# Self-attention in 32x32 diagonal blocks, with the block transposes on VectorE

## Chip, cores and metric

The kernel runs on one core of a Trainium2 chip. The metric is the device time of one execution in microseconds (us), as the median of several.

## What is computed

A pre-norm decoder layer on x of 16 x 128 x 1024 (2048 tokens), all fp32: self-attention, cross-attention with a context, and a feed-forward product, each added to its input. Only the self-attention matters here. It runs over the first axis, 16 long, so each of the 128 positions is a causal sequence of 16 tokens of its own:

```python
def _L0_attn_ref(tokens, weight_qkv, weight_proj):   # tokens: 16, 128, 1024
    NUM_HEADS, NUM_KV_HEADS, HEAD_DIM = (32, 8, 128)
    scale = 1.0 / HEAD_DIM ** 0.5
    qkv = jnp.einsum('sbh,ph->sbp', tokens, weight_qkv)
    ...
    k = jnp.repeat(k, Q_PER_GROUP, axis=2)           # 4 query heads share one k and one v
    v = jnp.repeat(v, Q_PER_GROUP, axis=2)
    ...
    scores = jnp.einsum('bhsd,bhtd->bhst', q, k) * scale
    causal = jnp.tril(jnp.ones((S, S), dtype=bool))
    scores = jnp.where(causal, scores, jnp.finfo(scores.dtype).min)
    attn = jax.nn.softmax(scores, axis=-1)
    out = jnp.einsum('bhst,bhtd->bhsd', attn, v)
    out = out.transpose(2, 0, 1, 3).reshape(S, B, NUM_HEADS * HEAD_DIM)
    return jnp.einsum('sbe,he->sbh', out, weight_proj)

x = x + _L0_attn_ref(_layernorm(x, axis=-1), L0_attn_weight_qkv, L0_attn_weight_proj)
```

## The kernel before

The 2048 tokens are laid out so that the 16 tokens of a sequence are neighbours. They form 4 blocks of 512, each of 4 tiles of 128 tokens; a tile holds 8 sequences. Of the 128x128 scores of a tile and head only 8 diagonal blocks of 16x16 are wanted; the mask `causal` sets the rest to -1e30.

`self_attention_phase` is a software pipeline of 33 steps (`pipeline`, line 271): a block has 8 groups (one k, one v and four q heads), and step n projects group n while it does the attention of group n-1. Step 0 has no attention, step 32 no projection. Inside a block, steps run two at a time in a hardware loop. Each engine has its own instruction list, written out by hand in `step`, and semaphores tie them together. The parts of a step:

- `unit(u)`, u from 0 to 5: projection of k, v and the four q heads for 512 tokens into the PSUM pair `u_ps`, 8 chunks of 128 features with three matmuls each. All large products are done in three passes (`three_passes`, line 48): an fp32 operand is split into a high part (rounded to fp32r) and a low part (the remainder), and high x high, high x low and low x high are summed.
- The splits: ScalarE (ACT) copies a weight tile to its high part (`weights`, line 598; `out_weights`, line 647), GpSimd (POOL) subtracts to get the low part (lines 436 and 447). POOL's order in a step: four splits of output weights (`sa_pl`, line 450), the projection weights of units 3, 4, 5 of this step, and those of units 0, 1, 2 of the next (`sa_wl`, line 439). `unit(u)` waits for its split on `w_split` (line 484).
- `scores(t)`, tile t: four plain fp32 matmuls of 128x128 into bank `s_ps` (line 521).
- `softmax(t)` on VectorE (DVE), lines 735 to 752: mask, maximum, subtract, then exp on ACT (`exps`, line 655), sum, reciprocal, multiply, 512 elements each in `probs`.
- `turn_probs(t)`: four 128x128 transposes on TensorE (PE) into bank `t_ps` (line 531), split by ACT (line 665) and DVE (line 756) into `probsTh` and `probsTl`.
- `mix_values(t)`: the product with v in three matmuls into `o_ps`; its split is `high_o` on ACT (line 671) and `low_o` on DVE (line 761), in one buffer `oh`/`ol`.
- `project(t)`: output projection of 4 heads, 2 halves of 512 columns, 24 matmuls, added to `acc` by DVE (`add_projected`, line 768). It needs all four output weight splits (`p_split`).
- `turn_v` transposes v (line 496); `fold_half` prepares weights of cross-attention (line 507).

The order on PE (lines 558 to 589) places a pair of turn and scores between the units, and `project(0)`, `mix_values(1)`, `turn_probs(2)` and `scores(3)` between `turn_v` and `unit(3)`. On ACT (lines 673 to 701) `out_weights([0, 1])` stands before `exps(0)`.

Of the kernel before, what the change touches and what calls it, by code (L numbers as in the profile page):

```python
# [13 lines left out]
P = 128  # L14
# [15 lines left out]
SELF_SCALE = 1.0 / HD ** 0.5  # L30

# [12 lines left out]
def f32(ap):  # L44
    return ap.bitcast(F32)
# [18 lines left out]
def constants_phase(nc, sems, ident, causal, pairmask, mix, bias_qkv, eps, b_nat, inter_rows, amp_col):  # L64

    with ExitStack() as ctx:
# [13 lines left out]
        slotmask = sb("slotmask", [P, SLOTS])  # L80
        bias_ps = ctx.enter_context(nc.psum_tensor("bias_ps", [P, HALF], F32))
# [15 lines left out]
        def _(pool):  # L97
# [9 lines left out]
                               pattern=[[-1, P]], channel_multiplier=1).then_inc(masks_built, 1)  # L107
# [7 lines left out]
            pool.affine_select(out=cv, in_=cv, compare_op=ALU.is_ge, fill=MASKED, base=SEQ - 1,  # L115
                               pattern=[[SEQ, P // SEQ], [0, SEQ]], channel_multiplier=-1).then_inc(masks_built, 1)
# [6 lines left out]
        def _(dve):  # L123
# [5 lines left out]
                                    ALU.add).then_inc(mix_steps, 1)  # L129
            dve.wait_ge(small_loaded, 48)  # L130
# [162 lines left out]
def self_attention_phase(nc, sems, ident, causal, mix, eps, x_rows, wqkv, wproj, w_nat, w_folded, x1):  # L293
# [7 lines left out]
    with ExitStack() as ctx:  # L301
# [22 lines left out]
        probs = sb("sa_probs", [P, QPG, P])  # L324
        probsTh = sb("sa_probsTh", [P, QPG * P], F32R)
        probsTl = sb("sa_probsTl", [P, QPG * P], F32R)
        top = sb("sa_top", [P, QPG])
        total = sb("sa_total", [P, QPG])
        inv = sb("sa_inv", [P, QPG])
        oh = sb("sa_oh", [P, QPG * P], F32R)  # L330
        ol = sb("sa_ol", [P, QPG * P], F32R)
# [5 lines left out]
        s_ps, t_ps, o_ps, v_ps = bank("sa_s"), bank("sa_t"), bank("sa_o"), bank("sa_vt")  # L337
        turn_ps = [s_ps, t_ps, o_ps, v_ps]
# [20 lines left out]
        inv_done = sem("sa_inv_done")  # L359
        probs_ready = sem("sa_probs_ready")  # L360
        probs_turned = sem("sa_probs_turned")
        probsT_hi = sem("sa_probsT_hi")
        probsT_ready = sem("sa_probsT_ready")
# [68 lines left out]
        def _(pool):  # L432
            pool.sem_inc(w_split, 3)
            pool.sem_inc(p_split, QPG)

# [26 lines left out]
        def _(pe):  # L462
            pe.sem_inc(pr_done, 1)
            pe.sem_inc(folded, 2)

# [9 lines left out]
            def step(s):  # L475
# [36 lines left out]
                def scores(t):  # L512
                    if not s.attn:
                        return
                    if t == 0:
                        pe.wait_ge(u_copied, n * U + 2)
                        if s.cross:
                            pe.wait_ge(ln.lo_done, s.b * ln.GROUPS + 5)
                    pe.wait_ge(s_masked, m * TILES + (t + 1))
                    for h in range(QPG):  # L520
                        ins = nc.tensor.matmul(s_ps[:, h * P:(h + 1) * P], qT[:, mp, h, t * P:(t + 1) * P],
                                               kT[:, mp, t * P:(t + 1) * P], start=True, stop=True)
                    ins.then_inc(s_done, 1)

                def turn_probs(t):
                    if not s.attn:
                        return
                    pe.wait_ge(probs_ready, m * TILES + (t + 1))
                    pe.wait_ge(probsT_ready, m * TILES + (t + 1))
                    for h in range(QPG):  # L530
                        ins = nc.tensor.transpose(t_ps[:, h * P:(h + 1) * P], probs[:, h], ident[:])
                    ins.then_inc(probs_turned, 1)

                def mix_values(t):
                    if not s.attn:
                        return
                    if t == 0:
                        pe.wait_ge(v_copied, v0 + 1)
                    pe.wait_ge(probsT_ready, m * TILES + (t + 2))
                    pe.wait_ge(o_split, m * TILES + (t + 1))  # L540
                    three_passes(nc, o_ps[:], [(vh[:, mp, t], vl[:, mp, t], probsTh[:], probsTl[:])]
                                 ).then_inc(o_done, 1)

                def project(t):
# [4 lines left out]
                    pe.wait_ge(o_split, m * TILES + (t + 2))  # L549
                    for half in range(2):  # L550
# [3 lines left out]
                                           [(oh[:, h * P:(h + 1) * P], ol[:, h * P:(h + 1) * P],  # L554
# [3 lines left out]
                scores(0)  # L558
                unit(0)
                turn_probs(0)  # L560
                scores(1)
                unit(1)
                mix_values(0)
                turn_probs(1)
                scores(2)
                unit(2)
                turn_v()
                project(0)
                mix_values(1)
                turn_probs(2)  # L570
                scores(3)
                unit(3)
                fold_half(0)
                project(1)
                mix_values(2)
                turn_probs(3)
                unit(4)
                fold_half(1)
                project(2)
                mix_values(3)  # L580
                unit(5)
                if s.norm:

                    pe.wait_ge(o_split, m * TILES + (TILES + 1))
                    pe.wait_ge(v_copied, v0 + 4)
                    turn_groups(s.b + 1, range(4))
                project(3)
# [6 lines left out]
        def _(act):  # L594
# [15 lines left out]
            def step(s):  # L610
# [44 lines left out]
                def exps(t):  # L655
                    if not s.attn:
                        return
                    act.wait_ge(s_shifted, m * TILES + (t + 1))
                    nc.scalar.activation(probs[:], probs[:], ACT.Exp, scale=SELF_SCALE).then_inc(exp_done, 1)

                def copy_probs(t):
                    if not s.attn:
                        return
                    act.wait_ge(probs_turned, m * TILES + (t + 1))
# [1163 lines left out]
```

## Time and profile before

| | us |
|---|---|
| median of 3 runs | 3785.24 |
| lowest, highest | 3785.0, 3787.38 |
| span of the profiled execution | 3789.7 |
| PE busy | 3586.1 (95%) |
| PE weight loads busy | 2841.5 (75%) |
| DVE busy | 1870.1 (49%) |
| ACT busy | 1315.5 (35%) |
| POOL busy | 1281.4 (34%) |

The profile is of one execution, and its own time is its span, from the first to the last instruction; it stands 4.5 us above the median. Busy time counts overlapping instructions once. Matmuls are pipelined: one that starts 0.23 us after its predecessor is recorded as 0.39 us long, so what a group costs is read from starts. Self-attention fills the first 2214 us, cross-attention and feed-forward the rest.

### The profile page before, as it was taken

The page shows a single profiled execution, that of the slowest core. Times are in us where ns is not written, and L with a number is a line of the kernel's source. Part 1 is how long each engine was busy: PE and PEld are TensorE (multiplying, and loading weights), DVE is VectorE, ACT ScalarE, POOL GpSimd, SP SyncE. Part 2 cuts the span into 40 slices and gives each one's busy share as a digit, 9 for nine tenths or more (in the row PEclk, how much of TensorE's full clock was granted, in tenths as well). Part 3 has the DMA queues.
Part 4 walks back from the last instruction along what each step waited for, and adds up shares of the span by engine and source line. Part 5 has one row for each costly group of instructions (what it writes and reads, how often), then busy time and mean ns, then how long its engine had stood idle before and what let it go on. Part 6 is the DMA issues. An engine that isn't in the chain of part 4 may idle for free. (4 is left out here: it accounts for less than half of the span.)

```text
span 3789.7 us, 51735 instructions
## 1 busy us (share of the span) xinstructions
PE 3586.1 (95%) x18740; PEld 2841.5 (75%) x18740; DVE 1870.1 (49%) x2810; ACT 1315.5 (35%) x1903; POOL 1281.4 (34%) x562
## 2 busy tenths in 40 slices
PE   6999999999999999999999869999999999997999
PEld 5888877888887888888878747777777777773487
DVE  3444364343453544445444435665665665652354
ACT  3233243333332323333233224454454544440100
POOL 4333343343433434334343333343343444320000
PEclk9999999999999999999999979999999999998899
DMA  4222233232323322323222144455546455443032
GB/s 172 78 100 94 84 132 123 89 105 83 113 98 123 111 84 99 115 79 139 72 88 72 34 146 125 128 162 159 141 145 173 132 155 168 128 109 156 21 129 83
DMA packets 137257, 431.21 MB, mean 114 GB/s; under 512 B 24112, under 2 KB 24112, under 8 KB 137144
## 3 DMA queue, kind: packets, MB, share of 16 engines
q1 hardware_dynamic: 131384, 408.58, 34.6%
q10 hardware_dynamic: 5760, 20.97, 1.4%
q8 instruction: 89, 1.46, 0.2%
q14 instruction: 24, 0.20, 0.0%
HBM read 316.21 MB, written 37.75 MB: 93 GB/s over the span
## 5 line engine op out<-in xcount | busy, mean ns | idle before, releaser
L439 POOL TENSOR_TENSOR sa_wl<-sa_wraw,sa_wh 128x1024 fp32r<-128x1024 f32 x192 | 472.5, 2468 | 1130.6 <-ACT sa_wh L601 1130.6
L51 PE MATMUL sa_u<-sa_ln_xh,sa_wh 128*128 128x512 f32 x1536 | 614.6, 400 | 3.9 <-DVE sa_ln_xl L248 3.9
L52 PE MATMUL sa_u<-sa_ln_xl,sa_wh 128*128 128x512 f32 x1536 | 599.0, 390 | 5.4 <-issue 5.4
L53 PE MATMUL sa_u<-sa_ln_xh,sa_wl 128*128 128x512 f32 x1536 | 600.9, 391 | 0.0
L768 DVE TENSOR_TENSOR sa_acc<-sa_pr,sa_acc 128x512 f32<-128x512 f32 x256 | 177.1, 692 | 827.4 <-PE sa_pr L53 827.3
L450 POOL TENSOR_TENSOR sa_pl<-sa_praw,sa_ph 128x1024 fp32r<-128x1024 f32 x128 | 336.0, 2646 | 239.3 <-ACT sa_ph L653 239.3
L51 PE MATMUL sa_pr<-sa_ph,sa_oh 128*128 128x512 f32 x1024 | 413.2, 404 | 2.5 <-DVE sa_ol L761 2.4
L52 PE MATMUL sa_pr<-sa_pl,sa_oh 128*128 128x512 f32 x1024 | 406.2, 397 | 0.0
L53 PE MATMUL sa_pr<-sa_ph,sa_ol 128*128 128x512 f32 x1024 | 405.3, 396 | 0.0
L53 PEld LDWEIGHTS sa_u<-sa_ln_xh,sa_wl 128*128 128x128 f32 x1536 | 288.9, 188 | 68.7 <-issue 5.8
L51 PEld LDWEIGHTS sa_u<-sa_ln_xh,sa_wh 128*128 128x128 f32 x1536 | 289.6, 189 | 59.7 <-issue 2.7
L52 PEld LDWEIGHTS sa_u<-sa_ln_xl,sa_wh 128*128 128x128 f32 x1536 | 289.7, 189 | 55.7
L1020 POOL TENSOR_TENSOR ca_wl<-ca_wraw,ca_wh 128x1024 fp32r<-128x1024 f32 x96 | 231.2, 2408 | 191.4 <-ACT ca_wh L1237 191.4
L1442 DVE TENSOR_TENSOR ca_acc<-ca_x,ca_acc 128x512 f32<-128x512 f32 x224 | 155.0, 692 | 193.6 <-PE ca_x L53 193.4
L51 PE MATMUL ca_u<-ca_ch,ca_wh 128*128 128x512 f32 x512 | 235.1, 459 | 12.1 <-POOL ca_cl L1026 12.1
L1020 POOL TENSOR_TENSOR ca_owl<-ca_wraw,ca_owh 128x1024 fp32r<-128x1024 f32 x33 | 78.6, 2383 | 484.6 <-ACT ca_owh L1237 484.6
L671 ACT ACTIVATE sa_oh<-sa_o 128x512 fp32r<-128x512 f32 x128 | 76.2, 595 | 477.6 <-PE sa_o L53 477.6
L51 PEld LDWEIGHTS sa_pr<-sa_ph,sa_oh 128*128 128x128 f32 x1024 | 193.4, 189 | 46.3 <-DVE sa_ol L761 3.3
L53 PEld LDWEIGHTS sa_pr<-sa_ph,sa_ol 128*128 128x128 f32 x1024 | 192.9, 188 | 46.8
L52 PEld LDWEIGHTS sa_pr<-sa_pl,sa_oh 128*128 128x128 f32 x1024 | 193.2, 189 | 42.5
L619 ACT ACTIVATE sa_qT<-sa_u 128x512 f32<-128x512 f32 x128 | 76.5, 597 | 412.0 <-PE sa_u L53 412.0
L1406 DVE TENSOR_REDUCE ca_top<-ca_s 128x8 f32<-128x1024 f32 x128 | 155.9, 1218 | 106.6 <-PE ca_s L1116 106.5
(195 smaller groups left out, 6750.7 us busy)
## 6 DMA issues: line engine op xcount, KB each, us to landing
sa_wraw<-in_wqkv SPq DMA_DIRECT2D x192, 512.0 KB, 3.5
sa_praw<-in_wproj SPq DMA_DIRECT2D x128, 512.0 KB, 3.5
ca_wraw<-w_folded SPq DMA_DIRECT2D x96, 512.0 KB, 3.3
ca_kstack<-ca_kmh SPq DMA_DIRECT2D x256, 128.0 KB, 2.4
ca_wraw<-in_wo SPq DMA_DIRECT2D x33, 512.0 KB, 4.2
ca_kstack<-ca_kml SPq DMA_DIRECT2D x128, 128.0 KB, 2.4
ca_qstack<-ca_qh SPq DMA_DIRECT2D x256, 64.0 KB, 2.6
sa_nat<-in_w_nat SPq DMA_DIRECT2D x24, 512.0 KB, 4.4
```

The lines of the kernel that those rows point to most:

```text
L51: nc.tensor.matmul(out, ah, bh, start=(first and i == 0), stop=False)
L52: nc.tensor.matmul(out, ah, bl, start=False, stop=False)
L53: ins = nc.tensor.matmul(out, al, bh, start=False, stop=(last and i == len(parts) - 1))
L439: nc.gpsimd.tensor_tensor(wl[:, u % 3], wraw[:, u % 3], f32(wh[:, u % 3]), ALU.subtract).then_inc(w_split, 1)
L450: nc.gpsimd.tensor_tensor(pl[:, h], praw[:, h], f32(ph[:, h]), ALU.subtract).then_inc(p_split, 1)
L619: nc.scalar.activation(dst[u], u_ps[u % 2][:], ACT.Copy).then_inc(u_copied, 1)
L671: nc.scalar.activation(oh[:], o_ps[:], ACT.Copy).then_inc(o_hi, 1)
L768: nc.vector.tensor_tensor(part, pr_ps[half][:], part, ALU.add).then_inc(pr_free, 1)
L1020: nc.gpsimd.tensor_tensor(low_weights[item], wraw[:, item % 2], f32(high_weights[item]), ALU.subtract).then_inc(w_split, 1)
L1406: nc.vector.tensor_reduce(top[:], s_ps[:].rearrange("p (s n) -> p s n", s=SLOTS), AX.X, ALU.max).then_inc(s_top, 1)
L1442: nc.vector.tensor_tensor(part, pr_bank(t, half)[:], part, ALU.add).then_inc(x_free, 1)
```

## The change

Only blocks of 32x32 on the diagonal of each 128x128 tile are computed; such a block holds two sequences and, with the mask in it, all that is wanted. A step's 4 tiles x 4 heads x 4 quadrants fit in one bank of PSUM, `s_ps`: 128 rows (quadrant and key) by 16 (tile and head) by 32 (query).

- `scores()` stands once per step, with 16 matmuls. Each has 32 columns of `kT` as weights and streams 4 x 32 columns of `qT`, and writes 32 rows of `s_ps`. Products lie keys by queries, hence the mask is transposed too (`causal_t`, 128 x 32).
- `softmax()` stands once per step: mask, a DVE transpose of each 32x32 block, maximum, subtract, exp, sum, reciprocal, multiply, and a second DVE transpose into `probsT`.
- `turn_probs` is gone, and so are its splits. In their place `spread_probs` on ACT copies each quadrant of 32 rows into the diagonal blocks of `diagh`, and `low_probs` on DVE writes the low part into `diagl`. Both tiles are 128 x 2048 and are set to zero once, by POOL at the start. `mix_values` takes 512 columns of them per tile, in the same three matmuls.
- The bank of the turns becomes a second `o_ps`; `oh` and `ol` are doubled, so `o_split` starts at 2.
- The orders change: on PE to scores, units 0 to 2, turn_v, mix 0, unit 3, fold, mix 1, project 0, unit 4, fold, mix 2, project 1, mix 3, unit 5, projects 2 and 3. On ACT `exps()` stands before `out_weights([0, 1])`, `spread_probs()` before `out_weights([2, 3])`. POOL's order within a step stays.

PE between two units of an ordinary step, before (`sa_t` is the bank of the turned probabilities, `sa_s` that of the scores, `sa_u` of the units):

```order
L53 MATMUL sa_u<-sa_ln_xh,sa_wl 128x512
L531 MATMUL sa_t<-ident,sa_probs 128x128 [waits sa_probsT_ready,sa_probs_ready]
L531 MATMUL sa_t<-ident,sa_probs 128x128 x3
L519 REGISTER_ALU
L521 MATMUL sa_s<-sa_kT,sa_qT 128x128 [waits sa_s_masked]
L521 MATMUL sa_s<-sa_kT,sa_qT 128x128 x3
L484 REGISTER_ALU
L51 MATMUL sa_u<-sa_ln_xh,sa_wh 128x512 [waits sa_u_copied,sa_w_split]
```

PE at the start of the step, after the change:

```order
L539 MATMUL sa_s<-sa_qT,sa_kT 32x128 [waits sa_s_masked,sa_u_copied]
L539 MATMUL sa_s<-sa_qT,sa_kT 32x128 x15
L498 REGISTER_ALU
L499 REGISTER_ALU [waits sa_ln_lo_done]
L500 REGISTER_ALU [waits sa_w_split]
L53 MATMUL sa_u<-sa_ln_xh,sa_wh 128x512 [waits sa_u_copied]
```

The pair between two units is gone: there the last matmul of a unit is followed by the first of the next. All scores stand in one group.

PE from the turn of V (`sa_vt`) to unit 3, after the change; before, the next unit behind the turn of V came after the 24 matmuls of `project(0)`, a mix, a turn and a score group:

```order
L511 MATMUL sa_vt<-ident,sa_vT 128x128 [waits sa_v_copied]
L511 MATMUL sa_vt<-ident,sa_vT 128x128 x3
L548 ISA [waits sa_v_copied]
L549 REGISTER_ALU [waits sa_diag_ready]
L53 MATMUL sa_o<-sa_diagh,sa_vh 128x512 [waits sa_o_split]
L54 MATMUL sa_o<-sa_diagl,sa_vh 128x512
L55 MATMUL sa_o<-sa_diagh,sa_vl 128x512
L499 REGISTER_ALU
L53 MATMUL sa_u<-sa_ln_xh,sa_wh 128x512 [waits sa_u_copied,sa_w_split]
```

Unit 3 and its wait for the weight split have moved forward past the project; `mix_values(0)` carries the wait for the spread tiles.

ACT at the start of the step, after the change (`sa_ph` are the high output weights, `sa_kT` the copy of unit 0); before, the rows of `sa_ph` stood in front of the row of `sa_probs`:

```order
L663 ACTIVATE sa_probs<-sa_probs 128x512 [waits sa_s_shifted]
L654 ISA
L656 REGISTER_ALU [waits sa_pr_done]
L657 ACTIVATE sa_ph<-sa_praw 128x1024 [waits sa_praw_loaded0]
L657 ACTIVATE sa_ph<-sa_praw 128x1024 [waits sa_praw_loaded1]
L622 ISA
L623 ACTIVATE sa_kT<-sa_u 128x512 [waits sa_u_done]
L604 ISA
L605 ACTIVATE sa_wh<-sa_wraw 128x1024 [waits sa_wraw_loaded0]
L670 ISA [waits sa_diag_zeroed]
L674 ACTIVATE sa_diagh<-sa_probsT 32x16x32 [waits sa_probs_turned,sa_o_done]
L674 ACTIVATE sa_diagh<-sa_probsT 32x16x32 x3
```

Exp now stands first, and the high parts of the spread tiles stand in front of output weights 2 and 3. The diff, cut to its core:

```diff
@@ constants_phase
+            for q in range(QUADS):
+                rows = slice(q * QW, (q + 1) * QW)
+                nc.vector.tensor_copy(causal_t[rows], causal[rows, rows])
@@ self_attention_phase, GpSimd
+            nc.gpsimd.memset(f32(diagh[:]), 0.0).then_inc(diag_zeroed, 1)
+            nc.gpsimd.memset(f32(diagl[:]), 0.0).then_inc(diag_zeroed, 1)
@@ TensorE
-                def scores(t):
...
-                    for h in range(QPG):
-                        ins = nc.tensor.matmul(s_ps[:, h * P:(h + 1) * P], qT[:, mp, h, t * P:(t + 1) * P],
-                                               kT[:, mp, t * P:(t + 1) * P], start=True, stop=True)
+                def scores():
...
+                    for t in range(TILES):
+                        for q in range(QUADS):
+                            rows = slice(q * QW, (q + 1) * QW)
+                            cols = slice(t * P + q * QW, t * P + (q + 1) * QW)
+                            ins = nc.tensor.matmul(s_ps[rows, t * P:(t + 1) * P], kT[:, mp, cols], qT[:, mp, :, cols],
+                                                   start=True, stop=True)
                     ins.then_inc(s_done, 1)
-                def turn_probs(t):
...
-                    for h in range(QPG):
-                        ins = nc.tensor.transpose(t_ps[:, h * P:(h + 1) * P], probs[:, h], ident[:])
@@ ScalarE
+                def spread_probs():
...
+                    act.wait_ge(diag_zeroed, 2)
+                    act.wait_ge(o_done, m * TILES + 1)
+                    act.wait_ge(probs_turned, m + 1)
+                    for q in range(QUADS):
+                        rows = slice(q * QW, (q + 1) * QW)
+                        nc.scalar.activation(diagh[rows, :, q], probsT[rows], ACT.Copy).then_inc(diag_hi, 1)
@@ VectorE, in softmax
+                    nc.vector.transpose(probs[:].rearrange("p k n -> p (k n)"),
+                                        masked[:].rearrange("p k n -> p (k n)")).then_inc(s_turned, 1)
...
+                    nc.vector.transpose(probsT[:].rearrange("p k n -> p (k n)"),
+                                        probs[:].rearrange("p k n -> p (k n)")).then_inc(probs_turned, 1)
+                def low_probs():
+                    dve.wait_ge(probs_turned, m + 1)
+                    for q in range(QUADS):
+                        rows = slice(q * QW, (q + 1) * QW)
+                        dve.wait_ge(diag_hi, m * QUADS + (q + 1))
+                        nc.vector.tensor_tensor(diagl[rows, :, q], probsT[rows], f32(diagh[rows, :, q]), ALU.subtract
+                                                ).then_inc(diag_ready, 1)
```

## Rows read from the trace of the kernel before

**Rows 1.** The page: busy us per engine, and granted PE clock in 40 slices.

```profile
PE 3586.1 (95%) x18740; PEld 2841.5 (75%) x18740; DVE 1870.1 (49%) x2810; ACT 1315.5 (35%) x1903; POOL 1281.4 (34%) x562
...
PEclk9999999999999999999999979999999999998899
```

**Rows 2.** Groups by line and shape, PE: records | busy us, mean ns | idle before.

```profile
L521 PE MATMUL sa_s<-sa_kT,sa_qT 128*128 128x128 f32 x1024 | 137.3, 278 | 1.4 <-ACT sa_qT L619 0.8 <-DVE sa_ln_xl L248 0.6
...
L1144 PE MATMUL ca_o_ps<-ca_probsT,ca_v 128*32 128x128 f32 x2048 | 83.3, 280 | 15.7 <-ACT ca_probsT L1298 12.9 <-issue 2.8
L531 PE MATMUL sa_t<-ident,sa_probs 128*128 128x128 f32 x512 | 80.6, 280 | 50.0 <-DVE sa_probs L751 50.0
```

**Rows 3.** Waits of PE: us in total, times, longest us.

```profile
PE sa_t L531 <- DVE sa_probs L751: 50.0, 52, 6.0
```

**Rows 4.** Timeline of PE, start of one step: start us, us busy, instruction.

```profile
751.88 1.05 PE L521 MATMUL sa_s<-sa_kT,sa_qT 128*128 128x128 f32 x8
752.68 0.47 PE L51 MATMUL sa_u<-sa_ln_xh,sa_wh 128*128 128x512 f32 x1
...
758.24 0.60 PE L531 MATMUL sa_t<-ident,sa_probs 128*128 128x128 f32 x4
758.67 1.06 PE L521 MATMUL sa_s<-sa_kT,sa_qT 128*128 128x128 f32 x8
759.49 0.48 PE L51 MATMUL sa_u<-sa_ln_xh,sa_wh 128*128 128x512 f32 x1
759.80 0.40 PE L52 MATMUL sa_u<-sa_ln_xl,sa_wh 128*128 128x512 f32 x1
```

**Rows 5.** Timeline of PE in cross-attention, a group of 32-column matmuls.

```profile
2500.48 0.65 PE L1144 MATMUL ca_o_ps<-ca_probsT,ca_v 128*32 128x128 f32 x16
2501.06 0.50 PE L51 MATMUL ca_u<-ca_ln_xh,ca_wh 128*128 128x512 f32 x1
2501.39 0.40 PE L52 MATMUL ca_u<-ca_ln_xl,ca_wh 128*128 128x512 f32 x1
```

**Rows 6.** Timeline of PE in the last step of self-attention, to its end.

```profile
2165.44 1.05 PE L521 MATMUL sa_s<-sa_kT,sa_qT 128*128 128x128 f32 x8
2172.48 1.11 PE L531 MATMUL sa_t<-ident,sa_probs 128*128 128x128 f32 x4 [5.99 <-DVE sa_probs L751]
...
2180.97 1.11 PE L531 MATMUL sa_t<-ident,sa_probs 128*128 128x128 f32 x4 [4.73 <-DVE sa_probs L751]
...
2213.94 0.39 PE L53 MATMUL sa_pr<-sa_ph,sa_ol 128*128 128x512 f32 x1
```

**Rows 7.** Timeline of ACT and DVE, two places: a table load, and the step of rows 4.

```profile
547.28 1.28 ACT L659 ACT_TABLE_LOAD   x1
549.38 0.63 ACT L659 ACTIVATE sa_probs<-sa_probs 128x512 f32<-128x512 f32 x1 [0.81 <-DVE sa_probs L744]
...
752.97 0.69 DVE L738 TENSOR_TENSOR sa_probs<-sa_s,causal 128x512 f32<-128x512 f32 x1 [0.20 <-PE sa_s L521]
...
753.43 2.01 ACT L653 ACTIVATE sa_ph<-sa_praw 128x1024 fp32r<-128x1024 f32 x2
...
755.35 0.61 ACT L659 ACTIVATE sa_probs<-sa_probs 128x512 f32<-128x512 f32 x1
...
756.93 0.99 DVE L751 TENSOR_TENSOR sa_probs<-sa_probs,sa_inv 128x512 f32<-128x512 f32 x1
...
758.43 0.60 ACT L619 ACTIVATE sa_kT<-sa_u 128x512 f32<-128x512 f32 x1 [2.47 <-PE sa_u L53]
758.93 1.05 ACT L601 ACTIVATE sa_wh<-sa_wraw 128x1024 fp32r<-128x1024 f32 x1
```

**Rows 8.** Timeline of POOL: first splits of the phase, and the step of rows 4.

```profile
21.17 6.94 POOL L439 TENSOR_TENSOR sa_wl<-sa_wraw,sa_wh 128x1024 fp32r<-128x1024 f32 x3 [18.02 <-ACT sa_wh L601]
...
754.57 5.59 POOL L450 TENSOR_TENSOR sa_pl<-sa_praw,sa_ph 128x1024 fp32r<-128x1024 f32 x2 [4.08 <-ACT sa_ph L653]
...
766.65 5.17 POOL L439 TENSOR_TENSOR sa_wl<-sa_wraw,sa_wh 128x1024 fp32r<-128x1024 f32 x2
```

More of the change, by code:

```diff
@@ L30 @@
 SELF_SCALE = 1.0 / HD ** 0.5
+QW = 32
+QUADS = P // QW
 CH = D // P
@@ L323, in self_attention_phase @@
         vl = sb("sa_vl", [P, 2, TILES, HD], F32R)
[L324 to L331, printed above, removed]
+        BLK = TILES * QPG
+        masked = sb("sa_masked", [P, BLK, QW])
+        probs = sb("sa_probs", [P, BLK, QW])
+        probsT = sb("sa_probsT", [P, BLK, QW])
+        diagh = sb("sa_diagh", [P, BLK, QUADS, QW], F32R)
+        diagl = sb("sa_diagl", [P, BLK, QUADS, QW], F32R)
+        top = sb("sa_top", [P, BLK])
+        total = sb("sa_total", [P, BLK])
+        inv = sb("sa_inv", [P, BLK])
+        oh = sb("sa_oh", [P, 2, QPG * P], F32R)
+        ol = sb("sa_ol", [P, 2, QPG * P], F32R)
         nat = sb("sa_nat", [P, D])
@@ L336, in self_attention_phase @@
         pr_ps = [bank(f"sa_pr{i}") for i in range(2)]
-        s_ps, t_ps, o_ps, v_ps = bank("sa_s"), bank("sa_t"), bank("sa_o"), bank("sa_vt")
-        turn_ps = [s_ps, t_ps, o_ps, v_ps]
+        s_ps, v_ps = bank("sa_s"), bank("sa_vt")
+        o_ps = [bank(f"sa_o{i}") for i in range(2)]
+        turn_ps = [s_ps, o_ps[0], o_ps[1], v_ps]
         wraw_loaded = [sem(f"sa_wraw_loaded{i}") for i in range(3)]
@@ L553, in project @@
                         ins = three_passes(nc, pr_ps[half][:],
-                                           [(oh[:, h * P:(h + 1) * P], ol[:, h * P:(h + 1) * P],
+                                           [(oh[:, t % 2, h * P:(h + 1) * P], ol[:, t % 2, h * P:(h + 1) * P],
                                              ph[:, h, cols], pl[:, h, cols]) for h in range(QPG)])
                         ins.then_inc(pr_done, 1)
-                scores(0)
+                scores()
                 unit(0)
-                turn_probs(0)
-                scores(1)
                 unit(1)
-                mix_values(0)
-                turn_probs(1)
-                scores(2)
                 unit(2)
                 turn_v()
[L568 to L571, printed above, removed]
+                mix_values(0)
                 unit(3)
                 fold_half(0)
-                project(1)
-                mix_values(2)
-                turn_probs(3)
+                mix_values(1)
+                project(0)
                 unit(4)
                 fold_half(1)
-                project(2)
+                mix_values(2)
+                project(1)
                 mix_values(3)
@@ L582, in step @@
                 if s.norm:
-                    pe.wait_ge(o_split, m * TILES + (TILES + 1))
+                    pe.wait_ge(o_split, m * TILES + (TILES + 2))
                     pe.wait_ge(v_copied, v0 + 4)
                     turn_groups(s.b + 1, range(4))
+                project(2)
                 project(3)
```

128 lines of the change are left out of this document (55 added, 73 removed).

## The prediction

> **What bounds the kernel now.** The page comes first: TensorE (PE) is busy 95% of the span and runs almost everywhere at the full granted clock [rows 1], the upper of its two levels (2.4 GHz). So an edit is worth what it takes out of PE's queue, plus what it takes out of PE's idle time, minus the waits it adds. Next come the groups by line and shape [rows 2]: the two groups that the change touches on PE are the scores (1024 records, 137.3 us busy) and the turns of the probabilities (512 records, 80.6 us). A score matmul of plain fp32 leaves two records, a turn leaves one. Third, PE's waits [rows 3]: in the self-attention steps one wait dominates, 50.0 us for probabilities that VectorE (DVE) has not finished, all in front of those turns. Last, the timeline of one step [rows 4], because busy time of overlapping short matmuls is not what they cost; starts are.
>
> There are 33 steps; 31 have both projections and attention, the first has no attention, and the last has no units. "S" below is the start of a step's first score matmul (751.88 in rows 4).
>
> **What goes from PE.** From start to start [rows 4]: the lone score group takes 752.68 - 751.88 = 0.80 us, a turn group 758.67 - 758.24 = 0.43, a later score group 759.49 - 758.67 = 0.82. The first unit matmul behind such a group starts its successor 0.31 later (759.49 to 759.80) where the usual pitch is 5.56/24 = 0.23 (unit 0, 752.68 to 758.24, 24 matmuls), so each switch costs another 0.08. Per step: one lone score group 0.88, three pairs of turn and score 3 x (0.43 + 0.82 + 0.08) = 3.99, one turn group alone 0.43: **5.30 us**.
>
> **What comes to PE.** One group of 16 matmuls of 128 rows by 32 columns that stream 128 columns, in four column strips in turn, so 32 records. The kernel before has this very form in cross-attention (line 1144): 2048 records, 83.3 us busy, 41 ns each, against 134 ns for the old scores [rows 2]. In the timeline 16 of them are busy 0.65 us, which is 15 pitches and one last record of 0.27, so 25 ns each; the next kind starts 0.58 us after the first of them [rows 5]. For 32 records I take 0.58 + 16 x 0.025 = 0.98, and 0.10 for the switch behind it (0.33 instead of 0.23, rows 5): **1.1 us**. The bounds: 1.0 if the switch costs nothing, and 3.3 (32 x 0.1025, the old pitch) if the strips do not overlap here. I stay with 1.1, as rows 5 have the same operand type and strip order; what differs is that qT is read in four pieces of 32.
>
> The switch deserves a second look. In rows 5 the next 128x128 matmul starts 0.07 us before the group's last record ends, and its successor follows after 0.33; behind the old groups it was 0.31. The Trainium skill, TensorEngine Tiling (Array Packing), Key Properties, says that changing the tiling mode drains TensorE. Taken as a full latency exposed on either side of the group, that would be about 0.5 us per step, 16 us in all, and the sum would be 16 us higher. The trace does not agree at that size, so the sum stays with the rows.
>
> Saved on PE: 31 x (5.30 - 1.10) = **130.2 us**.
>
> **The idle that goes.** The turns leave PE's queue, so the 50.0 us go as well [rows 3]; 5.99 and 4.73 of them lie in the last step [rows 6] and are counted there. The rest: **39.3 us**, 1.3 per step. Is the new wait later? mix_values(0) now needs the spread tiles. From S: mask starts at 1.09 (752.97; ScalarE (ACT) and DVE times from rows 7), then mask, transpose, top, subtract at a pitch of 0.72 each, exp starts at 3.97. From exp's start to the end of the multiplication it was 757.92 - 755.35 = 2.57; with a second transpose the turned probabilities are there at 7.3. ACT has put two output weight copies (2.01) and unit 0's copy and weight copy (until about 8.3) in front of the spread; four spread copies at 0.5 each end at 10.3, and the last low part on DVE at 11. PE reaches mix_values(0) only after three units (16.6) and the turn of V, at about 18. Cover of 7 us: no price. The extra work on DVE (two transposes, four low parts of 32 rows, for three softmaxes and four low parts fewer) is less than before. The DVE transpose has no row. Its floor is that of a 512-element operation, 0.69; above I allow double, 1.4, since the other 512-element operations of fp32 all take 0.69 [rows 7]. I take 0.7. The Trainium skill, VectorE: DVE Perf Modes, The three transpose paths, gives 311 ns for 128 columns of bf16; an estimate from it with one column per 0.96 GHz cycle is 0.71 us, and no run so far shows it.
>
> **What is late next.** Unit 3 moves forward. Before, a project (24 matmuls, 5.6 us) and a mix stood between the turn of V and unit 3 and hid the split of its weights; now only mix_values(0) does. PE arrives at S + 0.98 + 16.6 + 0.43 (turn of V) + 0.70 (three matmuls of 0.23) = 18.7. That split is the fifth operation of GpSimd (POOL) in the step: four output weight splits, then this one. Before, exp stood behind the first two output weight copies; now ACT waits for exp first. Exp ends at 4.6, the copy starts there, and the first split starts 1.14 later (754.57 - 753.43, rows 7, 8): 5.7. Two splits take 5.59, two more 5.17, the weight split half of that, 2.6 [rows 8], with output weights 2 and 3 copied just in time at 11.2: end at 19.0. Without DVE beside it three splits take 6.94 [rows 8], and DVE is idle from 11 on: end at 18.3. PE's wait lies between nothing and 0.3 us; I take 0.2, **6 us** in all. The table load in front of exp is no part of it, since it starts without waiting for the shift: at 547.28, with exp idle for another 0.81 behind it [rows 7].
>
> **The rest.** The last step runs from 2165.44 to 2214.3, 48.9 us [rows 6]. In the new one project(0) starts when the fourth output split ends, at 5.7 + 5.59 + 5.17 = 16.5; four projects at 24 x 0.235, two mixes and about 1 us at the lower clock make 42: **7 us** less. Two memsets on POOL lie in its 18.02 us of idle at the start [rows 8]: nothing. Four copies of the mask on DVE before the first barrier: 0.4 us at most. The edits of buffers and of the order of projects 1 to 3 remove no work and have their inputs some 10 us early: nothing. Cross-attention and FFN are untouched.
>
> **Sum.** 3789.7 - 130.2 - 39.3 - 7 + 6 + 0.4 = 3619.6 us for the profiled execution, whose span lies 4.5 us above the median of 3785.24; so **3615 us**, 4.5% less.
>
> **The rivals.**
> - *GpSimd sets the step.* The chain exp, output weight copies, splits ends 1 to 2 us after PE is at unit 3, since everything on it is in series and my margin is under half a us. For it: splits of 2.8 us beside DVE work, and exp moved ahead of the copies. Against: DVE is idle in the second half. Price 31 x (0.8 to 1.8) = 25 to 56 us more: 3640 to 3671.
> - *The column strips buy little.* The strided reading of qT, or a drain, brings the group to the old pitch of 3.3: 32 x 2.2 = 70 more, 3685. Against it stand rows 5. The page above would put the time at 3631 by its drain.
> - *The idle only moves.* PE waits as long at mix_values(0) as at the turns before: 39 more, 3654. Against: the 7 us of cover.
> - *Slower.* The first DVE transpose stands ahead of exp, hence ahead of the output weight copies, the five splits and unit 3. Each us of it over 0.7 delays unit 3 by one, 32 times. The gain of 176 us without the 6 is used up at (176/32) - 0.2 = 5.3 us over, a transpose of 6.0 us. At 8 us: 7.5 x 32 = 240, so 3849. For it: no row shows the operation. Against: nine times any 512-element row.
> - *The change doesn't do what it says:* excluded by the instruction lists, where the turns are gone and the scores stand once per step.
>
> **Chances.** Forecast 0.55, GpSimd 0.25, strips 0.10, idle moved 0.06, slower 0.04. The range 3598 to 3672 takes in the forecast (below it by a free switch, no wait at unit 3 and a cheaper last step), the moved idle and the GpSimd case; it leaves out the strips and slower. A measurement of this kernel tells 0.2% from no change. All cases but the last are over 1% faster: faster 0.95, same 0.01, slower 0.04.
>
> **What would show it.** Right: no turns of probabilities on PE; score records of about 40 ns busy each, one group of about 1 us per step; a step some 5.3 us shorter; PE's wait for probabilities gone and a wait of unit matmuls for POOL's weight split under 10 us in all. Wrong: that wait at 30 us or more (GpSimd); a score group of 2 to 3 us (strips); PE waiting for the low tiles (idle moved); a DVE transpose of well over 1 us.

## The result, and the profile after

The change makes the kernel faster, by clearly less than predicted.

| us | before | after |
|---|---|---|
| median | 3786.31 (4 runs) | 3681.61 (4 runs) |
| lowest, highest | 3785.0, 3788.86 | 3673.06, 3682.56 |
| span of the profiled execution | 3789.7 | 3678.7 |

The ratio is 0.9714, with a 95% interval from 0.9702 to 0.9727. The forecast of 3615 us was 67 us too low, and 3681.61 lies outside the range of 3598 to 3672. The sum for the profiled execution was 3619.6; it took 3678.7, so 59.1 us are to be found. (The other 7 us of the 67 are that the profiled span stood 4.5 us above the median before and stands 2.9 below it after.)

The page of the kernel after, lines that answer to [rows 1]:

```profile
PE 3449.9 (94%) x18228; PEld 2715.1 (74%) x18228; DVE 1551.2 (42%) x2302; ACT 1265.2 (34%) x1807; POOL 1258.1 (34%) x564
...
PEclk9999999999999999999999879999999999998999
```

PE has lost 136 us of work, yet it isn't busier by share. The groups of PE and DVE by line and shape in the kernel after, for the self-attention phase (us 60 to 2210), which answer to [rows 2]:

```profile
L539 PE MATMUL sa_s<-sa_qT,sa_kT 128*32 128x128 f32 x1024 | 36.7, 285 | 13.0 <-issue 12.1 <-ACT sa_qT L623 0.7
...
L756 DVE TENSOR_TENSOR sa_probs<-sa_probs,sa_inv 128x512 f32<-128x512 f32 x32 | 94.1, 2941 | 1.1
```

The turns of the probabilities are gone, and 1024 score records take 36.7 us where they took 137.3. The second row holds the surprise: the multiplication by the reciprocal takes 2.94 us. The waits of PE in the kernel after, which answer to [rows 3]:

```profile
PE sa_u L53 <- POOL sa_wl L453: 52.9, 31, 1.9
...
PE sa_o L53 <- issue: 12.5, 1, 12.5
```

The 50.0 us for probabilities have gone, and 52.9 us at unit 3 have come, in each of the 31 steps. The step that starts at 724.23 in the timeline of the kernel after, engine by engine; its PE rows answer to [rows 4], those of ACT and DVE to [rows 7], those of POOL to [rows 8]:

```profile
724.23 1.08 PE L539 MATMUL sa_s<-sa_qT,sa_kT 128*32 128x128 f32 x32
725.24 0.50 PE L53 MATMUL sa_u<-sa_ln_xh,sa_wh 128*128 128x512 f32 x1
...
742.05 0.48 PE L53 MATMUL sa_o<-sa_diagh,sa_vh 128*128 128x512 f32 x1
744.84 0.50 PE L53 MATMUL sa_u<-sa_ln_xh,sa_wh 128*128 128x512 f32 x1 [1.84 <-POOL sa_wl L453]
...
726.10 0.71 DVE L744 STREAM_TRANSPOSE sa_probs<-sa_masked 128x512 f32<-128x512 f32 x1
727.57 0.69 DVE L749 TENSOR_TENSOR sa_probs<-sa_probs,sa_top 128x512 f32<-128x512 f32 x1
729.97 2.94 DVE L756 TENSOR_TENSOR sa_probs<-sa_probs,sa_inv 128x512 f32<-128x512 f32 x1
732.94 0.71 DVE L759 STREAM_TRANSPOSE sa_probsT<-sa_probs 128x512 f32<-128x512 f32 x1
...
728.29 0.63 ACT L663 ACTIVATE sa_probs<-sa_probs 128x512 f32<-128x512 f32 x1 [12.10 <-DVE sa_probs L749]
733.75 2.59 ACT L674 ACTIVATE sa_diagh<-sa_probsT 32x512 fp32r<-32x512 f32 x4 [1.19 <-DVE sa_probsT L759]
736.36 2.01 ACT L657 ACTIVATE sa_ph<-sa_praw 128x1024 fp32r<-128x1024 f32 x2
...
729.95 5.22 POOL L464 TENSOR_TENSOR sa_pl<-sa_praw,sa_ph 128x1024 fp32r<-128x1024 f32 x2 [12.58 <-ACT sa_ph L657]
737.50 4.97 POOL L464 TENSOR_TENSOR sa_pl<-sa_praw,sa_ph 128x1024 fp32r<-128x1024 f32 x2 [2.33 <-ACT sa_ph L657]
742.43 7.02 POOL L453 TENSOR_TENSOR sa_wl<-sa_wraw,sa_wh 128x1024 fp32r<-128x1024 f32 x3
```

Read it as a chain. POOL's first split starts at 729.95, the multiplication 0.02 us later. Both inputs of the multiplication lie in SBUF, and it ends 0.35 us after half of POOL's 5.22, that is, after the first of the two splits. The second transpose is thereby at 732.94, the spread on ACT at 733.75, and output weights 2 and 3 stand behind it at 736.36. POOL has nothing to do for 2.33 us, its split for unit 3 ends at 742.43 + 7.02/3 = 744.77, and PE starts unit 3 at 744.84, 1.84 us late.

**Steps.** From score group to score group an ordinary step took 67.2 us before. After, in the first three blocks, it takes 63.0 or 64.6, and in the last block, where no weights are folded, 61.2 for 65.4. The window view of one step of the kernel before, and of two neighbouring ones of the kernel after (stretch, length, busy time of PE, its weight loads, DVE, ACT and POOL, granted clock, DMA share, GB/s):

```profile
751.90:819.10 67.20, 65.81 (x321) 54.56 (x320) 28.80 (x41) 22.67 (x32) 25.53 (x10) 1.00 0.28 93
```

```profile
724.20:788.90 64.70, 62.85 (x309) 51.35 (x309) 19.62 (x25) 19.84 (x28) 24.40 (x10) 0.97 0.27 97
788.90:851.90 63.00, 61.16 (x309) 50.14 (x308) 19.62 (x25) 21.12 (x29) 24.43 (x10) 1.00 0.28 100
```

The long steps are those in which the granted clock falls to the lower level (1.2 GHz) for a while. The PE timeline of such a step in the kernel after shows where:

```profile
872.50 0.69 PE L53 MATMUL sa_u<-sa_ln_xh,sa_wh 128*128 128x512 f32 x1 [1.85 <-POOL sa_wl L453]
872.98 0.63 PE L54 MATMUL sa_u<-sa_ln_xl,sa_wh 128*128 128x512 f32 x1
873.41 0.63 PE L55 MATMUL sa_u<-sa_ln_xh,sa_wl 128*128 128x512 f32 x1
```

Seven or eight matmuls start 0.43 us apart instead of 0.23, the first of them at most 1.5 us behind the wait. Nine ordinary steps (64.6 for 63.0 us) and three ends of blocks (68.3 for 66.6) have this, so 12 of the 31 steps are 1.65 us longer, 20 us in all. Behind 14 other waits of the same length (1.80 to 1.87 us) it doesn't fall.

### The profile page after: what moved, and what is told of

It is laid out like the page before. It is cut to its first block and busy times, and to the rows that moved or that the text cites. A ratio compares the mean times of both kernels' runs of the same rounds, so it can differ in the third digit from the quotient of the medians.

```text
span 3678.7 us, 49919 instructions
## 1 busy us (share of the span) xinstructions
PE 3449.9 (94%) x18228; PEld 2715.1 (74%) x18228; DVE 1551.2 (42%) x2302; ACT 1265.2 (34%) x1807; POOL 1258.1 (34%) x564
## 3 DMA queue, kind: packets, MB, share of 16 engines
q8 instruction: 87, 1.43, 0.2%
## 5 line engine op out<-in xcount | busy, mean ns | idle before, releaser
L453 POOL TENSOR_TENSOR sa_wl<-sa_wraw,sa_wh 128x1024 fp32r<-128x1024 f32 x192 | 457.3, 2395 | 756.9 <-ACT sa_wh L605 756.9
L53 PE MATMUL sa_u<-sa_ln_xh,sa_wh 128*128 128x512 f32 x1536 | 614.9, 400 | 57.0 <-POOL sa_wl L453 52.9
L54 PE MATMUL sa_u<-sa_ln_xl,sa_wh 128*128 128x512 f32 x1536 | 607.6, 396 | 0.0
L464 POOL TENSOR_TENSOR sa_pl<-sa_praw,sa_ph 128x1024 fp32r<-128x1024 f32 x128 | 325.1, 2561 | 524.5 <-ACT sa_ph L657 524.5
L53 PE MATMUL sa_pr<-sa_ph,sa_oh 128*128 128x512 f32 x1024 | 401.3, 392 | 1.6 <-POOL sa_pl L464 1.6
L772 DVE TENSOR_TENSOR sa_ol<-sa_o,sa_oh 128x512 fp32r<-128x512 f32 x128 | 88.2, 689 | 507.9 <-ACT sa_oh L680 507.9
L605 ACT ACTIVATE sa_wh<-sa_wraw 128x1024 fp32r<-128x1024 f32 x192 | 201.8, 1051 | 13.2 <-DMA sa_wraw<-in_wqkv 13.2
```

What stands on the lines that cost most here:

```text
L53: nc.tensor.matmul(out, ah, bh, start=(first and i == 0), stop=False)
L54: nc.tensor.matmul(out, ah, bl, start=False, stop=False)
L453: nc.gpsimd.tensor_tensor(wl[:, u % 3], wraw[:, u % 3], f32(wh[:, u % 3]), ALU.subtract).then_inc(w_split, 1)
L464: nc.gpsimd.tensor_tensor(pl[:, h], praw[:, h], f32(ph[:, h]), ALU.subtract).then_inc(p_split, 1)
L605: nc.scalar.activation(wh[:, u % 3], wraw[:, u % 3], ACT.Copy).then_inc(w_hi, 1)
L772: nc.vector.tensor_tensor(ol[:, t % 2], o_ps[t % 2][:], f32(oh[:, t % 2]), ALU.subtract).then_inc(o_split, 1)
```

## Experiments

**Theory A:** what is missing is the end of GpSimd's chain at unit 3; the multiplication sits beside a split and holds up spread, copies and splits in turn. **Rivals:** the score group or its switch costs more than rows 5 say; the buffers' new places changed something; the wait is of GpSimd's total work, so that no order removes it. Ratios are to the kernel before; the kernel after has 0.9714.

### Output weights ahead of the spread

```diff
-                spread_probs()
                 out_weights([2, 3])
+                spread_probs()
```

> The changed kernel with one edit on ScalarE: the copies of output weights 2 and 3 stand ahead of the four spread copies. Theory A (the multiplication on VectorE, stretched to 2.9 us beside the first output split on GpSimd, makes the spread late; output weights 2 and 3 stand behind the spread, so GpSimd idles 2.3 us before its third split and unit 3 waits 1.8 us): that idle goes, the wait of unit 3 falls from 52.9 us to under 10, the granted clock of the steps that stood at 0.97 returns to 1.00, and the span falls from 3678.7 to 3611 to 3622. Rival B (five splits in series are too long by themselves, whatever stands in front of them): the wait stays above 30 us and the span above 3655.

Measured: 3710.74 us, ratio 0.9797 [0.9781, 0.9814], slower than the kernel after. The wait at unit 3 went, as expected, and a longer one at mix 0 took its place, so the span came out at 3702.1 us where 3611 to 3622 was expected. Waits of PE in this kernel, and the timeline of POOL and DVE in one step:

```profile
PE sa_o L53 <- DVE sa_diagl L767: 66.2, 30, 3.8
```

```profile
76.60 10.83 POOL L464 TENSOR_TENSOR sa_pl<-sa_praw,sa_ph 128x1024 fp32r<-128x1024 f32 x4 [2.35 <-ACT sa_ph L657]
...
81.69 9.07 DVE L767 TENSOR_TENSOR sa_diagl<-sa_probsT,sa_diagh 32x512 fp32r<-32x512 f32 x4 [1.39 <-ACT sa_diagh L674]
```

POOL now runs without its gap, and the four low parts, whose inputs are both in SBUF too, take 9.07 us instead of 3.44: 2.3 us each, little less than one split of 2.71. The gap of 2.33 us in POOL had been what let them through. Half of theory A stands (the order causes the wait), but I had missed a second place of the same collision.

### The split for unit 3 between the output splits

`outs` runs the old loop body for the heads given to it; its definition is left out here.

```diff
-                    for h in range(QPG):
...
+                outs([0, 1])
+                if s.proj:
+                    weights(s.n, 3)
+                outs([2, 3])
...
-                    for u in range(3, U):
+                    for u in range(4, U):
```

> The changed kernel with one edit on GpSimd: the weight split of unit 3 stands between the second and the third output split. Theory A and rival B agree that unit 3 no longer waits; both expect the wait of unit 3 at nothing and no wait of project 0 for the output splits (they end near 20 us of the step, it starts at 27.7). Numbers: 31 steps lose 1.7 us (53 us); theory C (each stall of 1.8 us also costs the clock: steps with it last 64.6 instead of 63.0) adds some 10 steps of 1.6 us, so the span falls to 3605 to 3615. If the clock has nothing to do with the stall, some steps stay at 0.97 and the span is 3622 to 3628.

Measured: 3684.14, ratio 0.9722 [0.9703, 0.974], as the kernel after, span 3681.0: neither stretch of the expectation was met. The wait moved again; waits of PE, and the low parts in the groups of DVE:

```profile
PE sa_o L53 <- DVE sa_diagl L774: 53.4, 28, 2.0
```

```profile
L774 DVE TENSOR_TENSOR sa_diagl<-sa_probsT,sa_diagh 32x512 fp32r<-32x512 f32 x128 | 299.8, 2342 | 29.0 <-ACT sa_diagh L681 26.0
```

The split for unit 3 fills the gap that the low parts had used, and mix 0 waits 1.9 us for them. The clock falls behind 14 of these waits.

### GpSimd waits until the probabilities are turned

```diff
                 if s.attn:
+                    pool.wait_ge(probs_turned, s.m + 1)
                     for h in range(QPG):
```

> The changed kernel with one more wait: GpSimd starts its first output split only when the second transpose on VectorE is done, 1.5 us later than now. Theory A: alone, the multiplication takes 0.7 us instead of 2.9, the spread and output weights 2 and 3 come earlier, and although GpSimd starts later the wait of unit 3 falls from 1.8 to about 1.1 us; span 3640 to 3658. Rival B: the chain is as long as before and starts 1.5 us later, so the wait grows to 3.3 us and the span to 3720 or more.

Measured: 3691.88, ratio 0.9742 [0.9726, 0.9759], span 3699.9. Groups of DVE and waits of PE:

```profile
L768 DVE TENSOR_TENSOR sa_diagl<-sa_probsT,sa_diagh 32x512 fp32r<-32x512 f32 x128 | 304.1, 2376 | 61.6 <-ACT sa_diagh L675 58.6
L757 DVE TENSOR_TENSOR sa_probs<-sa_probs,sa_inv 128x512 f32<-128x512 f32 x32 | 22.1, 692 | 1.1
```

```profile
PE sa_u L53 <- POOL sa_wl L453: 36.6, 31, 1.3
PE sa_o L53 <- DVE sa_diagl L768: 20.9, 28, 0.8
```

This isolates the multiplication: with no split beside it, it takes 0.69 us instead of 2.94. The wait at unit 3 was as expected (1.2 us each for 1.1), and not the 3.3 of rival B. The wait at mix 0 (20.9 us in all) was not expected. With it, with the lower clock behind 16 of the 31 pairs of waits, and with 17.4 us of waiting in the last step instead of 12.5, the span missed the expected 3640 to 3658. POOL, started late, again runs its four splits without a gap, over all the low parts.

### Each output split as two halves

```diff
-                        nc.gpsimd.tensor_tensor(pl[:, h], praw[:, h], f32(ph[:, h]), ALU.subtract
+                        nc.gpsimd.tensor_tensor(pl[:, h, :HALF], praw[:, h, :HALF], f32(ph[:, h, :HALF]), ALU.subtract)
+                        nc.gpsimd.tensor_tensor(pl[:, h, HALF:], praw[:, h, HALF:], f32(ph[:, h, HALF:]), ALU.subtract
```

> The changed kernel with each output split on GpSimd made of two instructions of 512 columns. Theory F (VectorE waits for the end of one GpSimd instruction): the multiplication takes about 0.7 + 1.2 = 1.9 us instead of 2.9, the spread comes 1 us earlier, and unit 3's wait falls to about 0.9 us plus what the extra instructions cost GpSimd; span 3645 to 3665. If VectorE's operation is slowed in proportion while both run, the multiplication stays near 2.9 us and the span at 3679 or above.

Measured: 3660.71, ratio 0.9656 [0.9641, 0.9671]. Timeline of POOL and DVE in one step:

```profile
140.62 1.30 POOL L464 TENSOR_TENSOR sa_pl<-sa_praw,sa_ph 128x512 fp32r<-128x512 f32 x1 [12.58 <-ACT sa_ph L658]
...
140.63 1.83 DVE L757 TENSOR_TENSOR sa_probs<-sa_probs,sa_inv 128x512 f32<-128x512 f32 x1
...
143.97 6.64 DVE L768 TENSOR_TENSOR sa_diagl<-sa_probsT,sa_diagh 32x512 fp32r<-32x512 f32 x4 [0.76 <-ACT sa_diagh L675]
```

A multiplication that merely shared bandwidth with POOL would take as long beside halves as beside wholes. It takes 1.83 instead of 2.94 us: it waits for the end of one POOL instruction. The wait at unit 3 stayed at 50.4 us (31 times, 1.72 each as a rule) where 0.9 each and the cost of the extra instructions was expected: the multiplication gives 1.1 us, but the low parts now take 6.64 us, and eight halves on POOL last longer than four wholes. The time fell nevertheless, because in the first three blocks every ordinary step took 62.9 us, and only one step of the 31, in the last block, lost time to the clock. A step of that block without it and the one with it, in the window view of this kernel:

```profile
1814.90:1875.90 61.00, 59.28 (x289) 48.34 (x288) 21.71 (x25) 18.77 (x26) 26.11 (x15) 1.00 0.27 86
1936.00:1998.70 62.70, 60.95 (x289) 49.46 (x289) 21.62 (x26) 18.77 (x26) 26.09 (x15) 0.97 0.25 85
```

A wait of 1.7 or 1.8 us is thus not enough by itself for the lower clock; what decides it stays open.

### exp behind the first two output weights again

```diff
-                exps()
                 out_weights([0, 1])
+                exps()
```

> The changed kernel with ScalarE's first two output weight copies ahead of exp again, as before the change. Theory F (a VectorE operation with both inputs in SBUF waits for the end of the GpSimd operation in progress, and GpSimd's splits are 2.4 us each): the first two splits run from 1.5 to 6.7 us of the step and stretch the subtraction and the multiplication instead; the four low parts find GpSimd idle and stay at 0.8 us each. Unit 3's wait falls from 1.8 to about 0.6 us. Span 3620 to 3650. If the wait of unit 3 came from anything but the start of the GpSimd chain it stays at 1.8, 3679.

Measured: 3618.73 (3612.78 to 3623.36), ratio 0.9543 [0.9529, 0.9558], span 3621.4, as expected. Waits of PE:

```profile
PE sa_u L53 <- POOL sa_wl L453: 17.2, 31, 1.4
```

The wait is 0.37 us in most steps and 1.35 in six. Groups of DVE in this kernel:

```profile
L749 DVE TENSOR_TENSOR sa_probs<-sa_probs,sa_top 128x512 f32<-128x512 f32 x32 | 36.4, 1138 | 1.1
L756 DVE TENSOR_TENSOR sa_probs<-sa_probs,sa_inv 128x512 f32<-128x512 f32 x32 | 34.4, 1074 | 1.1
```

One line on ACT is worth 63 us. POOL starts earlier, its splits lie beside exp and the reductions, subtract and multiplication take 1.14 and 1.07 us on average, and all low parts fall into POOL's pause, at 0.68 us each. Ordinary steps of the first three blocks take 61.5 or 62.5 us, and none has the lower clock.

### POOL: the split for unit 3 early, then a gap for the low parts

The edit, against the kernel of the second experiment:

```diff
                 outs([0, 1])
                 if s.proj:
                     weights(s.n, 3)
+                if s.attn:
+                    pool.wait_ge(diag_ready, s.m * QUADS + QUADS)
                 outs([2, 3])
```

> The changed kernel with another GpSimd order and one more wait: output splits 0 and 1, weight split of unit 3, then a wait for the four low parts, then output splits 2 and 3, the rest as now. Theory F: GpSimd leaves VectorE a gap in which the low parts run, and unit 3's split is done near 13.5 us of the step. No wait of PE is left at mix 0 or unit 3, all ordinary steps last 61.2 us at a clock of 1.00, and the span falls to 3600 to 3612. If the stall only moves again (a fixed cost of this step), a wait of 1.8 us shows elsewhere and the span stays at 3680.

Measured: 3598.83 (3596.31 to 3603.55), ratio 0.9497 [0.9482, 0.9511], span 3598.7: as expected. POOL and DVE in one step of this kernel:

```profile
143.59 2.85 POOL L453 TENSOR_TENSOR sa_wl<-sa_wraw,sa_wh 128x1024 fp32r<-128x1024 f32 x1
148.58 4.75 POOL L466 TENSOR_TENSOR sa_pl<-sa_praw,sa_ph 128x1024 fp32r<-128x1024 f32 x2 [2.14 <-DVE sa_diagl L776]
...
142.87 5.55 DVE L776 TENSOR_TENSOR sa_diagl<-sa_probsT,sa_diagh 32x512 fp32r<-32x512 f32 x4 [0.76 <-ACT sa_diagh L683]
```

It differs from the second experiment in one wait, and is 85 us faster: POOL stands still for 2.14 us, the low parts pass, and PE waits neither at mix 0 nor at unit 3, except at mix 0 of the last step. All ordinary steps of the first three blocks take 60.9 us, as this one in the window view of this kernel:

```profile
132.67:193.57 60.90, 60.90 (x305) 50.23 (x304) 21.65 (x25) 21.25 (x29) 24.73 (x10) 1.00 0.30 104
```

The multiplication still takes 2.94 us here, so it costs only by what it delays. POOL's work is unchanged in sum, so the rival that POOL's total sets the step falls.

### Both, and both without the gap

On ACT as in the fifth experiment; on POOL as in the sixth, in the second kernel without its wait.

> Both good orders together: on ACT output weights 0 and 1 stand before exp again, and on POOL the order is outputs 0 and 1, the split for unit 3, a wait for the last low part of the probabilities, outputs 2 and 3, splits for units 4 and 5. Theory (the end of GpSimd's chain and its collision with DVE's two-SBUF operations are all that is lost): with the pool order alone neither unit 3 nor mix 0 waits any more, so moving exp can add nothing there; the step stays at 60.9 and the span within 3 us of the pool order alone, 3596 to 3602. Rival (the multiplication still costs PE something in that version, through the clock or late low parts): its mean falls from 2941 to about 1100 ns and the span goes below 3590.

> The same, without the wait for the low parts: POOL runs outputs 0 and 1, split for unit 3, outputs 2 and 3 as soon as their copies are there. Theory: the low parts (four DVE operations with both inputs in SBUF) run beside splits again only in part, since POOL has started 2 us earlier than with exp first; a wait at mix 0 of 0 to 1 us per step, span 3600 to 3630. Rival (starting early is enough, the gap isn't needed): no wait at mix 0, low parts under 1.4 us mean, span within 3 us of the run with the gap.

Measured: 3595.04 (3592.56 to 3600.16), ratio 0.9495 [0.9479, 0.951], span 3594.4 with the gap; 3597.24 (3593.18 to 3598.04), ratio 0.9496 [0.948, 0.9512], span 3595.4 without. Together with 3598.83 these are three versions that the measurement can't tell apart, all 2.3% under the kernel after. The ordinary step takes 60.9 us in all three. In the first the span lies 1.6 us under the expected stretch and above the rival's, although the multiplication is short there; its group in DVE:

```profile
L765 DVE TENSOR_TENSOR sa_probs<-sa_probs,sa_inv 128x512 f32<-128x512 f32 x32 | 34.4, 1075 | 1.1
```

So the 2.94 us cost nothing where the gap is. In the second the rival was right on the time and wrong on the low parts. Groups of DVE in that second kernel:

```profile
L774 DVE TENSOR_TENSOR sa_diagl<-sa_probsT,sa_diagh 32x512 fp32r<-32x512 f32 x128 | 243.2, 1900 | 40.3 <-ACT sa_diagh L681 37.3
```

They take 1.9 us each and cost nothing, since they start earlier in the step and end before PE is at mix 0, if only by 0.1 us (150.94 for 151.07 in the step that starts at 133.22). The gap is one way to get there, an earlier start of POOL another.

### The order of the column strips

```diff
-                    for t in range(TILES):
-                        for q in range(QUADS):
+                    for q in range(QUADS):
+                        for t in range(TILES):
```

> The changed kernel with the two loops of the score group exchanged: four matmuls in the same column strip follow each other before the next strip. If the 25 ns pitch comes from neighbours in different strips: the pitch rises to about 0.1 us, the group from 1.0 to 3.3 us, the span by 32 x 2.3 = 73 us to about 3750. If each 32-column matmul is simply short, or the queue finds the free strips by itself: no difference, 3679.

Measured: 3713.71, ratio 0.9794 [0.9777, 0.981], span 3718.1. Timeline of PE in this kernel:

```profile
136.16 2.46 PE L539 MATMUL sa_s<-sa_qT,sa_kT 128*32 128x128 f32 x32
138.55 0.50 PE L53 MATMUL sa_u<-sa_ln_xh,sa_wh 128*128 128x512 f32 x1
```

The same 32 records take 2.39 us from start to start when four matmuls in a row use one strip, and 1.01 when the strips alternate. So the overlap is real and depends on the order, by somewhat less than I expected (0.07 us per record for 0.10, and 3713.71 us for about 3750). The rival of costly scores falls: in the kernel after the group takes 1.01 us.

### The kernel before with its buffers shifted

```diff
+        gap = sb("sa_gap", [P, QPG])
```

> The kernel BEFORE with one more 32-byte buffer per partition allocated ahead of oh and ol, nothing else. Before, a project matmul follows the last one after 0.2345 us, in the changed kernel after 0.2288; units stand at 0.227 in both. Theory D (the pitch of the projects depends on where oh and ol start in SBUF: 32 bytes past a multiple of 64 in the changed kernel, on a multiple of 64 before): the pitch of the projects falls to 0.229 and the time by 3072 x 0.0057 = 17 us, ratio 0.9955. Rival E (it comes from the doubled buffer, or from less traffic of VectorE beside the matmuls): no difference, ratio 1.000.

Measured: 3786.2, ratio 0.9992 [0.9983, 1.0002]: no difference that these runs can tell. It was to explain why the matmuls of `project` are quicker after the change (below), and explains little of it: in the traces the last project of an ordinary step takes 5.59 us instead of 5.62, where the changed kernel has 5.49.

## Why the prediction was wrong

- **What goes from PE and what comes:** right. The new group takes 1.01 us with its first unit matmul 0.33 from its successor, 1.1 as taken; rows 5 were a good price for it. The old pairs are gone.
- **A term that I hadn't:** an ordinary step less its recorded wait is 63.0 - 1.84 = 61.16 us. Before it was 67.2 less 1.3 of idle, 65.9, and 5.30 off and 1.10 on made 61.7. The 0.54 more (17 us in 31 steps) lie in the projects: 24 matmuls there started 0.2345 us apart before and 0.2288 after, 0.14 us in each of four. I can't say why.
- **The idle that goes:** right. Mix 0 doesn't wait in ordinary steps. The cover was not the 7 us I had put down: with the multiplication at 2.94 the last low part ends at 13.6 from S, not at 11, and 4.2 are left. The first two experiments used them up.
- **What is late next, the step that failed.** Place and arrival were right: "PE arrives at S + 0.98 + 16.6 + 0.43 (turn of V) + 0.70 (three matmuls of 0.23) = 18.7", measured 18.8. The end of the split was not: "with output weights 2 and 3 copied just in time at 11.2: end at 19.0". Their copies started only at 12.1, and the split ended at 20.5. I had taken the step from exp's start to the end of the multiplication, 2.57 us, from rows 7, where the multiplication takes 0.99 us; in the changed kernel this stretch took 4.6. That row was itself partly beside a POOL split, and it contradicts my sentence that the other operations of 512 elements all take 0.69. The change places POOL's first split exactly over it, and the 2.94 us delay the spread, ACT's next copies, and so POOL itself, which idles 2.33 us in the middle of the chain that I had summed as without gaps. Instead of 6 us the wait is 52.9: 46.9 more.
- **The price of a wait:** I had priced it at its length. In 12 steps PE ran at the lower clock behind it: 20 us more, a term that the sum didn't have. At the full clock, too, it costs more than its length: the ordinary step of the sixth experiment, without a wait, takes 60.9 us, not 61.16. The idle time is counted from the recorded end of a matmul, 0.40 us behind its start, where the next would have started after 0.23, and the first matmul behind the wait starts its successor after 0.34. This is in the 61.16 already.
- **The rest:** last step 44.5 us (42 predicted, 48.9 before): +2.6, with 12.5 us of waiting for the spread tiles in it (the view puts them down to issue, but the last low part of that step ends at 2073.7 and mix 0 starts at 2073.8). The phase starts 1.8 us later. PE's idle time in the phase that the waits put down to issue is 12.1 us without the last step, and was 5.4: +6.7. It lies at two changes of block, where the score group now waits twice for about 3 us and a unit matmul had waited once; no run shows why.

46.9 + 20 - 17 + 2.6 + 1.8 + 6.7 = 61.0, of 59.1 to be found; of the -1.9 left, 1.4 lie behind self-attention (1575.4 us before, 1574.0 after).

The rival that GpSimd sets the step was the right one: 1 to 2 us late at unit 3, measured 1.7 on average. Its 3640 to 3671 ended 11 us under the measured median, since it too lacked the 20 us of the clock and the 6.7 at the changes of block, which the 17 that the projects gave back don't cover. I gave it 0.25, though my own two ends of the split, 18.3 and 19.0, lay on either side of PE's arrival at 18.7, behind a chain over three engines. Such a margin is no argument, and the profile had the warning in it. Groups of DVE of the kernel before, us 60 to 2210:

```profile
L744 DVE TENSOR_TENSOR sa_probs<-sa_probs,sa_top 128x512 f32<-128x512 f32 x128 | 182.5, 1426 | 4.5
...
L751 DVE TENSOR_TENSOR sa_probs<-sa_probs,sa_inv 128x512 f32<-128x512 f32 x128 | 117.9, 921 | 4.4
...
L756 DVE TENSOR_TENSOR sa_probsTl<-sa_t,sa_probsTh 128x512 fp32r<-128x512 f32 x128 | 87.6, 685 | 73.9 <-ACT sa_probsTh L665 73.9
```

Three operations of one shape: the one with an input in PSUM takes 0.69 us, the two that read SBUF twice 1.43 and 0.92 on average, with cases up to 2.8. The Trainium skill, SBUF — State Buffer, Who interferes with whom and Summary: rules for kernel authors, says that a VectorE instruction with two SBUF inputs contends with a GpSimd instruction that reads SBUF, and that the later one is blocked until the first finishes. The traces agree: 2.94 beside whole splits, 1.83 beside halves, 0.69 beside none. The delay is somewhat shorter than the recorded split: 2.25 us for 2.6, and 1.14 for 1.30. POOL is held up in its turn: the two splits beside the multiplication take 5.22 us, where three without DVE beside them took 6.94 [rows 8], 4.6 for two. The other rivals fell: the strips (2.3 us per step) and a slow DVE transpose (0.71, the 0.7 that I took).

## What to carry to other kernels

Where VectorE and GpSimd work in one step, list the VectorE operations that read two SBUF tensors and lay GpSimd's instructions over them: here each such operation that met a split waited for the end of one, so place them in GpSimd's pauses, or make a pause for them. A change that reorders queues moves these collisions, so a duration of such an operation may only be taken from a row with the same neighbour, with the free time (0.69 us here) and the blocked one (2.94) as its bounds. When a chain over several engines has a margin smaller than one such collision, the late case is the forecast; and what a wait costs is measured in step length, since PE may run slower behind it.

## What the hardware showed that I had not expected

- VectorE's reads of two SBUF tensors take turns with GpSimd: four low parts beside four splits in a row last 9.07 us, 2.3 each, about one per split, where they take 0.68 each in a pause. The second transpose (0.71) in the kernel after, the reductions (0.69) in that of the fifth experiment, and operations with an input in PSUM (0.69) take as long beside a split as without one.
- Behind a wait of 1.85 us PE ran seven or eight matmuls at a pitch of 0.43 us in 12 of 26 steps; with halved splits and waits of 1.68 to 1.75 us, in 1 of 26. Which it will be, no row here tells.
- Matmuls of 32 columns take 0.03 us per record when the four column strips alternate and 0.07 when a strip is used four times running.
- The three passes of `project` have means of 404, 397 and 396 ns in the kernel before and 392, 394 and 391 after. The nine variants of the kernel after have them too (within 1 ns), and the shift of the buffers by 32 bytes brings the kernel before only to 402, 395 and 395. The cause is open; no run has the doubled `oh` and `ol` alone.
